# Ranking stage of a graph network kernel: message sums by pairs of tiles, with selections and rank counts in between

## What is computed

```python
row, col = src, dst
B = jnp.exp(-edge_weight)
msgs = B[:, None] * x[col]
out = jax.ops.segment_sum(msgs, row, num_segments=N_NODES)
x = _layernorm(x + out)
```

## Time and profile before

| | us |
|---|---|
| median of three runs | 11174.61 |
| profiled execution, its own time | 11183.53 |
| its span, first to last instruction | 11181.7 |
| ranking stage, from its first rank count to the last scatter | about 2390 |
| VectorE busy in the span | 4736.9 (42%) |
| GpSimd busy in the span | 7106.9 (64%) |

### The profile page before, as it was taken

How to read it: one execution, slowest core, us unless ns; L and a number is a source line. 1 busy time by engine, 2 the same in 40 slices (tenths; PEclk the granted TensorE clock), 3 DMA queues, 4 the chain that set the end, 5 groups by cost and what they waited for, 6 DMA issues and landing times.

```text
span 11181.7 us, 57120 instructions
## 1 busy us (share of the span) xinstructions
PE 1801.6 (16%) x9285; PEld 1516.5 (14%) x9285; DVE 4736.9 (42%) x20005; ACT 1142.1 (10%) x2728; POOL 7106.9 (64%) x6884
## 2 busy tenths in 40 slices
PE   8744444444000400000000000000001000000000
PEld 7633333333000300000000000000000000000000
DVE  8855555555797422222221222222224344444446
ACT  0143434343000100000000000000000000000000
POOL 0566666666201377777776677777777776666766
PEclk7755555555555555555555555555555555555555
DMA  5144444444575111111111111111111222222221
GB/s 224 57 129 122 129 124 126 124 127 122 204 273 203 32 50 46 48 46 48 46 48 37 50 46 48 46 48 46 48 46 30 54 53 58 53 58 55 56 55 44
DMA packets 570444, 911.29 MB, mean 81 GB/s; under 512 B 333435, under 2 KB 348228, under 8 KB 544824
## 3 DMA queue, kind: packets, MB, share of 16 engines
q1 hardware_dynamic: 350264, 652.74, 17.3%
q0 software_dynamic: 219904, 255.88, 10.8%
HBM read 494.12 MB, written 414.02 MB: 81 GB/s over the span
## 4 chain that ended last, share of the span: by engine, by line
DVE 34%; issue 28%; another core or an unknown queue 17%; POOL 16%; PE 3%; DMA 1%; ACT 1%; DVEq 0%; SPq 0%; POOLq 0%; ACTq 0%
DVE arena_a L1495 16%; POOL arena_a L641 15%; DVE arena_b L1112 4%; DVE arena_a L1110 3%; DVE arena_b L1125 3%; DVE arena_a L1425 3%; POOL arena_a L610 2%; PE bank L811 2%; DVE arena_b L1056 1%; DVE arena_b L1093 1%; PE bank L916 1%; DVE arena_a L1625 0%; PE bank L890 0%; DMA arena_a<-in_a 0%
## 5 line engine op out<-in xcount | busy, mean ns | idle before, releaser
L641 POOL DMA_INDIRECT arena_a<-table_c,decay x3136 | 3284.6, 1047 | 1257.6 <-issue 1051.2
L1495 DVE SCALAR_TENSOR_TENSOR arena_a<-arena_a,same_dst 128x64 f32<-128x64 f32 x3134 | 891.5, 284 | 3449.5 <-DVE arena_a L1495 2713.2
L591 POOL DMA_INDIRECT by_src<-arena_b,idx_blk x1568 | 1570.8, 1002 | 885.8 <-issue 449.4
L641 POOL DMA_INDIRECT arena_a<-table_at,decay x1568 | 1556.8, 993 | 703.8 <-issue 468.4
L1110 DVE SCALAR_TENSOR_TENSOR arena_a<-arena_a,same_dst 128x64 f32<-128x64 f32 x1567 | 441.9, 282 | 711.1 <-remote 547.7
L864 PE MATMUL bank<-ident,chunk_end 128*64 128x128 f32 (+2 forms) x8 | 2.7, 442 | 4416.0 <-DVEq L973 4416.0
L864 PEld LDWEIGHTS bank<-ident,chunk_end 128*64 128x64 f32 (+2 forms) x8 | 1.4, 240 | 4416.6 <-DVEq L973 4416.6
L1112 DVE SCALAR_TENSOR_TENSOR arena_b<-arena_a,src_f,before 128x128 bf16<-128x128 f32 x1568 | 543.7, 347 | 37.4 <-issue 37.4
L850 PE MATMUL bank<-hrows 98*128 98x128 f32 x1568 | 404.0, 440 | 659.5 <-DVE arena_b L1125 331.9
L850 PE MATMUL bank<-hrows,arena_a 98*128 98x128 f32 x1568 | 403.3, 438 | 658.0 <-DVE arena_b L1125 347.4
L753 ACT ACTIVATE arena_b<-arena_a,decay 128x64 f32<-128x64 f32 x1568 | 394.2, 334 | 972.5 <-remote 610.2
(11 more groups left out here) (279 smaller groups left out, 4845.9 us busy)
## 6 DMA issues: line engine op xcount, KB each, us to landing
arena_a<-ids_rows SPq DMA_DIRECT2D x98, 1024.0 KB
states_src<-arena_a SPq DMA_DIRECT2D x98, 1024.0 KB
states_c<-arena_a SPq DMA_DIRECT2D x196, 512.0 KB
hrows<-by_src SPq DMA_DIRECT2D x98, 776.0 KB, 6.1
states_at<-arena_a SPq DMA_DIRECT2D x98, 576.0 KB
x_at_start<-arena_a SPq DMA_DIRECT2D x7, 7168.0 KB, 49.0
arena_a<-x_at_start SPq DMA_DIRECT2D x98, 512.0 KB
arena_a<-table_c,decay POOLq DMA_INDIRECT x3136
```

What stands on the lines that cost most here:

```text
L591: pool.indirect_dma_start(out=by_src, out_offset=AT(ap=idx_blk[r][:, k:k + 1], axis=0), in_=rows[r][:, k, :], in_offset=None)\
L641: pool.indirect_dma_start(out=gb[r][:, k * w:(k + 1) * w], out_offset=None, in_=table[g], in_offset=AT(ap=src_i[:, n * J + k:n * J + k + 1 ...
L1495: ins = v.scalar_tensor_tensor(out=st[h][:, k * D:(k + 1) * D], in0=old, scalar=same_dst[:, e:e + 1], in1=gb[r][:, k * D:(k + 1) * D], op0 ...
```

## The change

A pair is two neighbouring tiles, 2i and 2i + 1. The product of the two masks of each pair is made once, ahead of the stage (`both_same`, one instruction over 784 columns). For each pair there are now three message instructions in place of two:

- `pair_alone`: tile 2i + 1 = `xs` of 2i x mask + `xs` of 2i + 1. It needs nothing of the chain.
- `pair_joined`, first: tile 2i + 1 = old x product of masks + what `pair_alone` wrote.
- `pair_joined`, second: tile 2i = old x mask + `xs` of 2i. It raises `v_pairs`, on which the next pair waits, and on which ScalarE now waits as well.

The order of each pair is: `pair_alone` of the next pair, two selections of the block before, the wait on the last pair, the two joined instructions, and two rank counts. So the last thing before `positions` is now a rank count, where it was a selection. Two more scratch tiles (`junk`) take the outputs that nobody reads.

```diff
-                        act.wait_ge(s("v_tiles"), t + Q)
+                        act.wait_ge(s("v_pairs"), (t + Q) // 2)
...
+            masks = same_dst[:, :].rearrange("p (m two) -> p m two", two=2)
+            link(v.tensor_tensor(both_same, masks[:, :, 0], masks[:, :, 1], ALU.mult))
...
-                for k in range(q * Q, (q + 1) * Q):
-                    t = n * J + k
-                    old = xb[h][:, k - 1, :] if k else xb[1 - h][:, J - 1, :] if n else first_row[:, :]
-                    if t:
-                        v.wait_ge(s("v_tiles"), t)
-                    v.scalar_tensor_tensor(out=xb[h][:, k, :], in0=old, scalar=same_dst[:, t:t + 1],
-                                           in1=xs[h][:, k, :], op0=ALU.mult, op1=ALU.add).then_inc(s("v_tiles"), 1)
...
+            def pair_alone(n, i):
+
+                h, t = n % 2, n * J + 2 * i
+                ins = v.scalar_tensor_tensor(out=xb[h][:, 2 * i + 1, :], in0=xs[h][:, 2 * i, :],
+                                             scalar=same_dst[:, t + 1:t + 2], in1=xs[h][:, 2 * i + 1, :],
+                                             op0=ALU.mult, op1=ALU.add)
+                if i == 0:
+                    ins.then_inc(s("pair_begun"), 1)
+
+            def pair_joined(n, i):
+
+                h, t, pair = n % 2, n * J + 2 * i, n * (J // 2) + i
+                old = xb[h][:, 2 * i - 1, :] if i else xb[1 - h][:, J - 1, :] if n else first_row[:, :]
+                if pair:
+                    v.wait_ge(s("v_pairs"), pair)
+                v.scalar_tensor_tensor(out=xb[h][:, 2 * i + 1, :], in0=old, scalar=both_same[:, pair:pair + 1],
+                                       in1=xb[h][:, 2 * i + 1, :], op0=ALU.mult, op1=ALU.add)
+                v.scalar_tensor_tensor(out=xb[h][:, 2 * i, :], in0=old, scalar=same_dst[:, t:t + 1],
+                                       in1=xs[h][:, 2 * i, :], op0=ALU.mult, op1=ALU.add).then_inc(s("v_pairs"), 1)
...
-                for q in range(J // Q):
+                if n < NBLK:
+                    pair_alone(n, 0)
+                for i in range(J // 2):
+                    if n < NBLK and i + 1 < J // 2:
+                        pair_alone(n, i + 1)
+                    if n:
+                        select(n - 1, 2 * i)
+                        select(n - 1, 2 * i + 1)
                     if n < NBLK:
-                        stage_a(n, q)
-                    if n:
-                        stage_b(n - 1, q)
+                        if i == 0:
+                            v.wait_ge(s("pair_begun"), n + 1)
+                        pair_joined(n, i)
+                        rank_of(n, 2 * i)
+                        rank_of(n, 2 * i + 1)
```

More of the change, by code:

```diff
@@ new lines, in rank_of, with select @@
+            def rank_of(n, k):
+                h, t = n % 2, n * J + k
+                rank = v.scalar_tensor_tensor(out=junk[2 + Q + k % 2 if k % 4 > 1 else k % 2], in0=ids_in[h][:, k * P:(k + 1) * P],
+                                              scalar=src_f[:, t:t + 1], in1=before[:, :],
+                                              op0=ALU.is_equal, op1=ALU.mult, accum_out=rank_blk[:, h, k:k + 1])
+                if k == J - 1:
+                    rank.then_inc(s("ranked"), 1)
+            def select(n, k):
+                q, h, group = k // Q, n % 2, n * (J // Q) + k // Q
+                if k % Q == 0:
+                    v.wait_ge(s("counted"), group + 1)
+                    if group:
+                        v.wait_ge(s("selected"), group)
+                chosen = v.scalar_tensor_tensor(out=junk[2 + k % Q], in0=p_cnt[q][:, k % Q * P:(k % Q + 1) * P],
+                                                scalar=1.0, in1=one(oh_lo[h], k), op0=ALU.mult, op1=ALU.mult,
+                                                accum_out=sel_blk[:, h, k:k + 1])
+                if k % Q == Q - 1:
+                    chosen.then_inc(s("selected"), 1)
```

21 lines of the change are left out of this document (3 added, 18 removed).

## The result

The changed kernel takes 11290.03 us, median of 4 runs (11283.73 to 11299.47), against 11182.24 us (11172.26 to 11193.84, 4 runs) for the kernel before on the same chip: a ratio of 1.0094, 95% interval 1.0078 to 1.0110. It is 0.9% slower. The forecast was 11252 us, 0.7% slower, range 11040 to 11340. Sign, size and range held. The mechanism behind the size did not, as the experiments show: it was that of the rival which I had given 0.12.

What follows compares the result with a forecast made beforehand. It took the scatter stage as bound by GpSimd's issuing plus a 3.62 us wait per block for VectorE. 96 gaps x 0.8 = +77 us on 11183.5 gave 11260; with the median 8.9 us lower, 11252 us, range 11040 to 11340.

Steps and rivals of the forecast that it cites:

- the rival which I had given 0.12: Scatter stage: all eight `pair_alone` a block paid at 0.20 us after VectorE's slow stretch, 157 us, giving 11332; chance 0.12.
- the gap is the only thing at stake: Scatter stage: only GpSimd's 3.62 us wait between blocks can be gained or lost, of which about 0.3 stays.
- A rate, not a latency: Late in a block, VectorE records complete about every 0.75 us whether they wait or not; semaphore delay between sums isn't the cost.
- The length of the slow part: VectorE's stretch of slow completions ends 2.54 us after the last scatter issue; forecast 11.9 us instead of 12.73, holding 16 records.
- the sum: Scatter stage's total: 96 gaps, each growing 0.8 us, +77 us; bounds +38 and +106.
- As it is the loads that hold the scatters back: SyncE's loads keep VectorE fast at a block's start, so its slow stretch begins 11.61 us after the load.
- the growth of the gap: GpSimd's wait between blocks grows by 0.8 us, with 9 records left after VectorE's slow stretch; 0.4 to 1.1 possible.
- a fast part too long: VectorE's fast stretch at a block's start was to last 9.57 us instead of 8.72 and hold 61 to 67 records.
- ScalarE's four scalings end the gap: Block's end: GpSimd starts when ScalarE's four scalings after the last joined sum end; 1.87 us, against 1.80 by the index block.
- what would show it: Expected: GpSimd's wait 3.6 to 4.4 us, issue gaps over all lines, 16 to 17 slow records, load 0.4 us before GpSimd.
- the first rival: Scatter stage: the signal from sum to sum is the cost, so GpSimd's gap closes to 0.3 us: 317 us less, 10858; chance 0.30.

Runs made afterwards that it cites:

- The 24 records less of chip 4: Kernel before with each group's four selections made as one product and one reduction, 56 records a block instead of 80: 11350.44 us, ratio 1.0153.
- chip 2's three kernels of an even gap: Kernel before with eight unread VectorE instructions more a block (1.0095), with sums not waiting for each other (1.0004), or with pairs in the old order (1.0132).

## Why the prediction came out right, and where it was wrong

**That the gap is the only thing at stake: right.** The stage took 110.0 us more, the gaps between blocks 120.6 (123.3 less the 2.7 before the first block), and GpSimd's own issuing a little less (20.50 us a block in the mean, 20.61 before); the other stages took nothing.

**A rate, not a latency: right, and shown.** The chain loosened gives 1.0004, eight records more 1.0095. The rule of the Trainium skill that the prediction weighed, to minimize operations and not semaphores ("VectorE: DVE Perf Modes", § Rules for kernel authors), is borne out for the slow part by these two ratios, as far as one goes in a kernel that keeps its gap. The 24 records less of chip 4 (1.0153) and the new order with its 80 (1.0093) show where it ends.

**The length of the slow part: right in form.** It ends 2.56 us after the last scatter, as in the sum (2.54). It was to be 11.9 us with 16 records and was 12.77 with 19, counted alike (17.9 in the mean over the blocks), because it began earlier than I put it.

**"As it is the loads that hold the scatters back": this step failed.** I took the 11.61 us from the load to the slow part as fixed, though the same rows gave a second distance, 10.39 us from GpSimd's first scatter. With the load 0.41 us ahead of GpSimd instead of 1.22, the two part: 11.61 from the load would be 11.20 from GpSimd, and it was 10.28. The kernel with fewer loads (10.38, ratio 0.9993; as fast at 66 GB/s), that with one load more (10.38 in the median, as slow at 245 GB/s; 1.0035) and the block without a pause, where loads give no fast part, settle it together. None of them would alone: the first keeps the ids.

**What follows from that step in the sum.** Not 61 to 67 of the new block's records fit into the fast part but 56. By the right distance: fast part 10.39 - 1.67 = 8.7 us, as before; slow part 20.58 + 2.54 - 10.39 = 12.7 us, as before. So nothing but the end of the block has room for eight more records. I put 9 behind the slow part where 5 were; counted alike it is 13 in the block shown, and 13.6 against 5.5 in the mean over the blocks.

**The term that was mis-sized, the growth of the gap: 0.8 us, measured 1.24** (120.6 over 97). Of it 1.10 us lie between the slow part's end and GpSimd's start (1.25 to 2.35 in the mean), the rest before, as the slow part ends 2.58 us behind the last scatter in the mean where it was 2.40. The records behind the slow part run at 1.56 / 11 = 0.142 us each, eight of them 1.13 us, and 96 x 1.13 = 109 us. Measured are +107.8 in the medians and +110.0 in the stage; that these lie so near is in part chance, as the gaps grew by 120.6 and shorter issuing took some 11 off. This is the second rival, "the records are paid in full", with its own mechanism; only its price was wrong, as it took 0.20 us a record, that of a sum, where the mix of the block's end costs 0.14. It would have given 11284 with that. I held the likeliest mechanism to be another and came within 38 us by luck: a fast part too long made the 0.8 too small, and a wait put down to ScalarE added 0.07 to it (1.87 against 1.80).

**That ScalarE's four scalings end the gap: wrong.** The four scalings at a block's end are of the block that VectorE is summing, and the scatters then due are of the block before. Those wait for scalings that, by their records, had ended 24.4 us earlier in the median (25.3 in the changed kernel). In the block after, the index block ends at 1530.48 + 0.17, its signal takes 0.28, and GpSimd starts at 1530.93, to the hundredth; the scalings, by their record, end at 1531.04, later than the start. The row of the kernel before that I had not read says the same:

```profile
1528.02 0.17 DVE L1137 TENSOR_TENSOR idx_blk<-rank_blk,sel_blk 128x16 int32<-128x16 f32 x1
```

1528.02 + 0.17 + 0.28 = 1528.47, the start in the earlier trace rows. GpSimd starts 0.27 or 0.28 us behind the index block's end in 95 of 96 blocks before and 94 of 96 after. So VectorE's last records set GpSimd's start in both kernels, and each record behind the slow part counts in full. With 4 records from 1527.39 to positions before and 12 from 1528.77 now, 0.55 us became 1.63, which is the block's 1.09 us more from the end of the slow part to GpSimd's start (1.08 before, 2.17 now).

**Three signs out of "what would show it" came**: issue gaps over all lines, the joined sums no more than others, SyncE's load 0.41 us before GpSimd. The two numbers in it that hung on the loads, 4.4 us and 16 to 17 records, came out as 4.7 and 5.0 us in the block shown (the mean over the blocks is 4.9) and 19 (17.9).

**What none of the terms had: the pause can't be closed.** The sum and the first rival let the gap shrink to 0.3 us. In the traces with the slow part a pause below some 2 us costs the next block its fast part (the table above), so the 10858 us of that rival can't be had by closing the gaps. My estimate of the most that could be had is 96 x (3.6 - 2.0), about 150 us.

**What stays open.** Why the new order alone costs 0.9%: its records are those of before. A gap under 1.8 us and the long one behind it are explained by the table; why this order gets to such gaps, and the changed kernel with the same order does not, is not known. Why pairs cost more in the old order (1.0132) than eight idle records (1.0095). Why the parts don't add. So eight records as the cause of the loss rest on the changed kernel's own trace (8.1 records more behind the slow part) and on the equal ratio of the eight idle ones on another chip, not on a sum of parts. And what on the chip slows VectorE's completions: the writing of the rows' contents is excluded, issuing and the packets' handling are not told apart.

## What to carry to other kernels

Count an engine's records, not its waits, where its gaps are labelled "issue" at a steady distance: a wait that is taken away there comes back in front of the next instruction, and added records are paid behind the slow stretch, each at its ordinary pace. The reverse isn't safe: fewer records (1.0153) can close a gap that the next block lives on. When a stretch seems to begin at a fixed distance from some event, measure the distance from every candidate event in the same rows, and ask which one the change moves apart; two candidates that start together explain nothing until they are parted. And try a change of this size on more than one chip before its mechanism is believed: the same kernel had another bound on one chip.

## What the runs showed of the hardware

- The same program took 10092 us on one chip and 11107 to 11182 us on the others, 10% apart. On the one, VectorE has no slow part beside GpSimd's indirect DMAs, in this stage (88.9 us of waiting, once). The gathers of the later stages differ too: their issues are shorter (L642 946 ns a piece against 1047), and VectorE's chained sums wait for the DMA (2894.5 us) and not for each other (2669.3). I know of no row that tells why.
- On the others, VectorE's records complete at about one each 0.7 us in the slow part of GpSimd's scatters (0.70 to 0.71 us apart where they are even; 17 records in 12.73 us before, 19 in 12.77 after), whether they depend on each other or not, until some 2.5 us after the last scatter. This goes on when 4 of each row's 388 bytes travel.
- The first issue gap comes 10.3 to 10.4 us after GpSimd resumes, in the median of the blocks before, after, with fewer loads and with one more; in chip 2's three kernels of an even gap it is 10.2 to 11.6. It needs a pause of GpSimd: in the new order alone 29 blocks with pauses up to 1.76 us have no fast part, and 66 with pauses from 1.98 us on have it in full. The gap of this kernel is so in part what makes it run: VectorE gets a block done in time only because GpSimd waited for the one before.
